# Four sets of expert-row buffers, a straight attention stage, and integer row numbers written by a reduction, in a graph-attention and mixture-of-experts kernel

## The reference

```python
def gnn(x, adj, W, a):                       # 4 heads of 32
    h = (x @ W).reshape(B, N, 4, 32).transpose(0, 2, 1, 3)
    s1, s2 = einsum('bhnd,hd->bhn', h, a1), einsum('bhmd,hd->bhm', h, a2)
    e = leaky_relu(s1[..., None] + s2[:, :, None, :], 0.2)
    e = where(adj[:, None] == 0, -inf, e)
    return softmax(e) @ h                    # back to 128 features

def ffn(x, Wg, bg, W1, b1, W2, b2):          # 8 experts, the best 2 of each token
    scores, idx = top_k(x @ Wg.T + bg, 2)
    p = softmax(scores)
    return sum over the 2 experts e of p_e * (relu(x @ W1[e].T + b1[e]) @ W2[e].T + b2[e])

x = x + gnn(layernorm(x), adj, W, a)
x = x + ffn(layernorm(x), Wg, bg, W1, b1, W2, b2)
```

## Time and profile before

| what | us |
|---|---|
| median of three runs | 736.47 (729.72 to 737.64) |
| the profiled execution | 735.45 |
| its span, first to last instruction | 733.6 |
| mean granted TensorE clock (share of full speed) | 0.852 |

### The profile page before, as it was taken

The page is one execution under the profiler, slowest core; times in us unless marked ns, Lnnn a source line. Parts: engine busy times, 40 slices in busy tenths (PEclk is TensorE's granted clock), DMA queues, the critical chain, the costliest instruction groups (busy, mean ns, idle before and its releaser), DMA issues.

```text
span 733.6 us, 23123 instructions
## 1 busy us (share of the span) xinstructions
PE 527.0 (72%) x7450; PEld 471.8 (64%) x7509; DVE 543.2 (74%) x1566; ACT 443.5 (60%) x908; POOL 430.7 (59%) x384
## 2 busy tenths in 40 slices
PE   1798878888887898886210888798888978888200
PEld 1598768887777888876210677687777867767100
DVE  4598999887999989988468566656746765666277
ACT  1788867756777786662132665566656656656064
POOL 2344487875888787786465166555655755564500
PEclk9999998968999888898655799999998999999755
DMA  8712122320333332000415222222222222221099
GB/s 308 270 60 60 60 84 78 88 84 23 86 86 86 83 79 83 25 28 31 143 40 106 60 68 70 74 67 63 79 64 65 75 68 61 69 71 49 7 356 331
DMA packets 60760, 67.64 MB, mean 92 GB/s; under 512 B 7266, under 2 KB 46317, under 8 KB 60416
## 3 DMA queue, kind: packets, MB, share of 16 engines
q1 hardware_dynamic: 41936, 44.31, 20.0%
q0 software_dynamic: 8816, 17.46, 7.3%
q10 hardware_dynamic: 9920, 4.73, 2.4%
HBM read 44.16 MB, written 23.22 MB: 92 GB/s over the span
## 4 chain that ended last, share of the span: by engine, by line
PE 47%; DVE 20%; issue 16%; DMA 6%; another core or an unknown queue 4%; ACT 4%; POOL 1%; DVEq 1%; ACTq 1%; SPq 0%; POOLq 0%
PE bank L1413 15%; PE bank L1401 13%; PE bank L1233 6%; PE bank L1224 3%; DVE bs L676 2%; PE bank L1389 2%; PE bank L1262 2%; DVE G L790 1%; DMA adji<-expert_out 1%; PE bank L1255 1%; DVE mv L679 1%; DVE T L799 1%; ACT G L549 1%; POOL expert_rows L467 1%
## 5 line engine op out<-in xcount | busy, mean ns | idle before, releaser
L517 POOL DMA_INDIRECT expert_out<-ysb,bidx x142 | 165.4, 1164 | 129.0 <-DVE ysb L1159 71.3
L467 POOL DMA_INDIRECT expert_rows<-rowt,idx x128 | 154.4, 1206 | 61.7 <-issue 34.5
L549 ACT ACTIVATE G<-bank,s2c 128x512 uint8<-128x512 f32 x256 | 154.3, 696 | 10.3 <-remote 9.8
L1233 PE MATMUL bank<-V,G 128*128 128x66 bf16 x3072 | 141.0, 202 | 14.5 <-issue 11.0
L1413 PE MATMUL bank<-W2h,G 128*128 x1704 | 122.6, 228 | 33.2 <-issue 29.9
L646 ACT ACTIVATE h<-bank,b1s,sc 128x256 f32<-128x256 f32 x284 | 138.0, 569 | 13.5 <-PE bank L1401 8.3
L1233 PEld LDWEIGHTS bank<-V,G 128*128 128x128 fp8e4 x3072 | 129.3, 103 | 18.5 <-issue 11.7
L1413 PEld LDWEIGHTS bank<-W2h,G 128*128 128x128 f16 x1704 | 107.2, 102 | 51.4 <-issue 50.2
L1401 PE MATMUL bank<-xt,W1h 128*128 128x256 f16 x852 | 113.5, 282 | 7.1 <-issue 6.7
L639 ACT ACTIVATE xt<-bank 128x512 f16<-128x512 f16 x71 | 43.0, 605 | 95.7 <-remote 79.3
L1142 DVE CAST G<-h 128x1024 f16<-128x1024 f32 x71 | 54.1, 762 | 58.9 <-ACT h L646 57.0
(11 more groups left out here) (159 smaller groups left out, 795.0 us busy)
## 6 DMA issues: line engine op xcount, KB each, us to landing
adji<-in_adj SPq DMA_DIRECT2D x16, 1024.0 KB
xb<-expert_rows SPq DMA_DIRECT2D x71, 130.0 KB
G<-in_L_ffn_W SPq DMA_DIRECT2D x2, 2048.0 KB, 9.3
adji<-expert_out SPq DMA_DIRECT2D x8, 512.0 KB, 5.6
G<-expert_out SPq DMA_DIRECT2D x8, 512.0 KB, 7.6
expert_out<-ysb,bidx POOLq DMA_INDIRECT x142
expert_rows<-rowt,idx POOLq DMA_INDIRECT x128
out<-adji ACTq DMA_DIRECT2D x8, 256.0 KB, 6.8
```

The source lines that it names most:

```text
L467: pool.indirect_dma_start(xs, bass.IndirectOffsetOnAxis(ap=idx[:, Z.p, k, j:j + 1], axis=0), rowt[:, Z.p, j, :], None).then_inc(scattered[ ...
L517: pool.indirect_dma_start(ybuf, bass.IndirectOffsetOnAxis(ap=bidx[:, B.o, t:t + 1], axis=0), ysb[:, B.q, t, :], None, bounds_check=2 * TOK ...
L549: act.activation(Gs[:, M.p, h // 2, mt, :, h % 2], zb[h][:, :], ACT.Sign, bias=s2c[:, M.p, mt, h:h + 1]).then_inc(S["z_used"], 1)
L1233: last = mm(o[:, h, :], G8[:, R.p, h // 2, mt, nt * P:(nt + 1) * P, h % 2], v[:, h, :], start=False, stop=(part == H and mt == NT - 1 and ...
```

## The change

What it does: `rowt` and `idx` get four sets instead of two, with four semaphores that count the scatters, and the waits for their reuse look four batches back. `slots` loses its loop; every slot of the attention stage is straight code on all four engines, so that every register expression in it becomes a constant. `slotf` and the step `indices` are gone: `places` reduces `prod` by a maximum straight into the int32 `idx`, after the wait for the scatters. The two copies into the row buffer become reductions by a maximum over a dimension of length one. `PLACE_STEPS` is 9, and two waits that count its steps follow. The expert stage and SP's own loop over the adjacency loads are as they were.

```diff
-LN_STEPS, ..., PLACE_STEPS = 8, 5, 2, 6, 2, 4, 13, 10
+LN_STEPS, ..., PLACE_STEPS = 8, 5, 2, 6, 2, 4, 13, 9
...
-        slotf = sb("slotf", [P, 2, NT])
-        idx = sb("idx", [P, 2, 2, NT], I32)
-        rowt = sb("rowt", [P, 2, NT, ROW])
+        idx = sb("idx", [P, 4, 2, NT], I32)
+        rowt = sb("rowt", [P, 4, NT, ROW])
...
-        scattered = [S["scattered0"], S["scattered1"]]
+        scattered = [S[f"scattered{k}"] for k in range(4)]
...
         def slots(eng, body, ahead, behind):
-            start = behind + 3
-            pairs = (NB - ahead - start) // 2
...
-            for s in range(-ahead, start):
-                body(fixed(s))
-            with eng.Fori(0, pairs) as i:
-                for u in range(2):
-                    body(looped(u, i))
-            for s in range(start + 2 * pairs, NB + behind):
-                body(fixed(s))
+            for s in range(-ahead, NB + behind):
+                at = lambda k, s=s: Batch(s + k) if 0 <= s + k < NB else None
+                at.s = s
+                body(at)
...
-            sp.wait_ge(scattered[0], 16 * 2 * NT * NB // 2)
-            sp.wait_ge(scattered[1], 16 * 2 * NT * NB // 2)
+            for k in range(4):
+                sp.wait_ge(scattered[k], 16 * 2 * NT * NB // 4)
...
             def weights(Z):
-                ge(act, S["place_steps"], Z.n * PLACE_STEPS - 4)
+                ge(act, S["place_steps"], Z.n * PLACE_STEPS - 3)
...
             def high_rows(Q):
-                ge(act, scattered[Q.p], Q.h * 16 * 2 * NT)
-                act.activation(rowt[:, Q.p, :, 0:D // 2].bitcast(FP16), xn2[:, :, :], ACT.Copy) \
+                ge(act, scattered[Q.q], Q.f * 16 * 2 * NT)
+                act.activation(rowt[:, Q.q, :, 0:D // 2].bitcast(FP16), xn2[:, :, :], ACT.Copy) \
...
             def places(Z):
-                pc.did(dve.tensor_reduce(slotf[:, :, :], prod[:, :, :, :], AX.X, ALU.add))
-                ge(dve, scattered[Z.p], Z.h * 16 * 2 * NT)
-                pc.did(dve.tensor_copy(rowt[:, Z.p, :, D + 1], v01[:, 0, :]))
-                pc.did(dve.tensor_copy(rowt[:, Z.p, :, D], C(C_TOK)[:, bass.ds(Z.n * NT, NT)]))
-
-            def indices(Z):
-                pc = Chain(dve, S["place_steps"], PLACE_STEPS, Z.n)
-                pc.k = 9
-                pc.after(7)
-                pc.did(dve.tensor_copy(idx[:, Z.p], slotf[:, :, :]))
+                ge(dve, scattered[Z.q], Z.f * 16 * 2 * NT)
+                pc.did(dve.tensor_reduce(idx[:, Z.q], prod[:, :, :, :], AX.X, ALU.max))
+                pc.did(dve.tensor_reduce(rowt[:, Z.q, :, D + 1], v01[:, 0, :].unsqueeze(2), AX.X, ALU.max))
+                pc.did(dve.tensor_reduce(rowt[:, Z.q, :, D], C(C_TOK)[:, bass.ds(Z.n * NT, NT)].unsqueeze(2),
+                                         AX.X, ALU.max))
...
                 if m1:
                     scaled_sums(m1, 0)
-                if m4:
-                    indices(m4)
```

More of the change, by code:

```diff
@@ L151 @@
 PIECES = 4
-LN_STEPS, S_STEPS, MX_STEPS, ARG_STEPS, X_STEPS, ATT_STEPS, ROUTE_STEPS, PLACE_STEPS = 8, 5, 2, 6, 2, 4, 13, 10
+LN_STEPS, S_STEPS, MX_STEPS, ARG_STEPS, X_STEPS, ATT_STEPS, ROUTE_STEPS, PLACE_STEPS = 8, 5, 2, 6, 2, 4, 13, 9
 def build(nc, x, adj, W, a, Wg, bg, W1, b1, W2, b2, const, out):
@@ L314, in build @@
             ln2 rstd2 nb2_ready xn2_ready x2T_ready xn2T_ready gate_ready route_steps dm_ready place_steps ed_ready rank_ready
-            hi_ready lo_ready scattered0 scattered1 tab_steps ends_ready tab_ready pads_ready
+            hi_ready lo_ready scattered0 scattered1 scattered2 scattered3 tab_steps ends_ready tab_ready pads_ready
             ld_rows0 ld_rows1 ld_rows2 ld_rows3 bt_ready xt_ready up_ready hid_ready split_steps down_ready y_ready
@@ L333, in slots @@
         def slots(eng, body, ahead, behind):
-            start = behind + 3
-            pairs = (NB - ahead - start) // 2
-            def fixed(s):
-                at = lambda k: Batch(s + k) if 0 <= s + k < NB else None
+            for s in range(-ahead, NB + behind):
+                at = lambda k, s=s: Batch(s + k) if 0 <= s + k < NB else None
                 at.s = s
[L339 to L344, removed]
-            for s in range(-ahead, start):
-                body(fixed(s))
-            with eng.Fori(0, pairs) as i:
-                for u in range(2):
-                    body(looped(u, i))
-            for s in range(start + 2 * pairs, NB + behind):
-                body(fixed(s))
+                body(at)
         def blocks(eng, body):
@@ L467, in scatter @@
                     pool.indirect_dma_start(
-                        xs, bass.IndirectOffsetOnAxis(ap=idx[:, Z.p, k, j:j + 1], axis=0),
-                        rowt[:, Z.p, j, :], None).then_inc(scattered[Z.p], 16)
+                        xs, bass.IndirectOffsetOnAxis(ap=idx[:, Z.q, k, j:j + 1], axis=0),
+                        rowt[:, Z.q, j, :], None).then_inc(scattered[Z.q], 16)
             def low_rows(Q):
                 hold(pool, S["hi_ready"], Q.n + 1, S["pool_turns"])
-                pool.tensor_tensor(rowt[:, Q.p, :, D // 2:D].bitcast(FP16), xn2[:, :, :],
-                                   rowt[:, Q.p, :, 0:D // 2].bitcast(FP16), ALU.subtract) \
+                pool.tensor_tensor(rowt[:, Q.q, :, D // 2:D].bitcast(FP16), xn2[:, :, :],
+                                   rowt[:, Q.q, :, 0:D // 2].bitcast(FP16), ALU.subtract) \
                     .then_inc(S["lo_ready"], 1)
@@ L828, in low_rows @@
                 dve.wait_ge(S["hi_ready"], Q.n + 1)
-                dve.tensor_tensor(rowt[:, Q.p, :, D // 2:D].bitcast(FP16), xn2[:, :, :],
-                                  rowt[:, Q.p, :, 0:D // 2].bitcast(FP16), ALU.subtract).then_inc(S["lo_ready"], 1)
+                dve.tensor_tensor(rowt[:, Q.q, :, D // 2:D].bitcast(FP16), xn2[:, :, :],
+                                  rowt[:, Q.q, :, 0:D // 2].bitcast(FP16), ALU.subtract).then_inc(S["lo_ready"], 1)
             def stats2(R, half):
```

## The result

Over 20 runs of each on one chip the changed kernel takes 725.87 us (median; 714.72 to 729.73), the kernel before 729.44 (724.42 to 737.64). The ratio is 0.9882, 95% interval 0.9853 to 0.9911: 8.6 us faster. The medians of all runs lie only 3.6 us apart. The forecast was 9 us. By the ratio the size came out; much of the way to it did not.

A forecast was written before the change was run, and what follows sets the result against it. No single engine led all twelve attention slots; DVE's copies waited for POOL. Slot gains, limited by POOL's and PE's own work, summed to 8.7 us, rounded 9: median 736.5 to 727.5 us, own range 721 to 733, 8 in 10 712 to 738.

The forecast's parts named there:

- reductions that do not wait: DVE's row edits: small reductions run undisturbed by GpSimd at 0.15 to 0.21 us each, argued from L983.
- rival D: DVE's new reductions wait as the copies did, so only the order changes: 736 us; chance 0.06.
- straight code at 0: Attention slots without the loop: register work saved is not visible, bounds -0.3 to +0.3 us for eight slots each.
- Rival C: Fetching straight code stalls PE, DVE or ACT from 150 to 318 us; 13 more pages cost 14 us: 742; chance 0.08.
- The walk of `edges` into `low_part`: DVE's L782 starts earlier and meets GpSimd's L457: up to some tenths of a microsecond per slot, not in the sum.
- the slots led by DVE: Attention slots where DVE was the chain: two like 215.87 give 1.4 us each, the one at 108.98 gives 1.9.
- the four PE-led ones: Four attention slots like the one at 276.50, bound by PE with its stalls: 0, at most 0.9 us each.
- The first slot: The attention slot at 89.09, where only the `idx` conversion stood: 19.89 to 18.4 us, a gain of 1.5.
- rival A: DVE and POOL led everywhere; PE's stalls and half clock come from late feeding; twelve slots give 28 us: 708; chance 0.22.
- the three waits of 7.4, 22.4 and 8.1 us: DVE's L985, L986 and L993 in the attention stage: 48 tiny instructions, 30.2 us of it standing still, 2.5 per slot.
- the four sets at 0: ACT's L598 waited 2.2 us in all for landed scatters; four sets give between 0 and 2.2 us, taken as 0.
- a sign against itself: A gain lying behind 340 us, after the attention stage, where the forecast gave nothing, would show it wrong.

The follow-up runs named there:

- The two halves: The kernel before with the int32 reduction alone, 1.0002, and the kernel before with the two row reductions alone, 0.9978; both on the second chip.
- the version at 0.972: The changed kernel with its two one-long reductions turned back into copies: 0.9722 to the kernel before on the third chip, 0.9813 on the fourth.

## Why the prediction was right, and where it was not

**Right.** The prices: reductions that do not wait, 0.21, 0.15 and 0.15 us; nothing more for an int32 result (rival D is out); GpSimd's wait for `idx` gone from the twelve slots; straight code at 0, shown alone at 0.997 where TensorE does not stall. DVE's busy time over twelve slots fell by 31.9 us, a little more than the 22 to 30 given. Rival C, code fetch, did not come: the instruction queue carries 66 packets in place of 52 (the forecast said some 13 more), and the one long "issue" wait, 5.6 us, stood in the kernel before as well. The walk of `edges` into `low_part`, no term of the sum, cost next to nothing on the two chips with stalls: L767 takes 1219 ns in the mean on the first, as before (1218), and 1318 on the second.

The proof that a reduction does not wait was weaker than it reads in the forecast. L983 starts 0.20 us after the scatter, and at 0.24 a copy doesn't wait either. The ten reductions named above, at 0.33 or 0.34 us, show it.

**Right in size, wrong in place: the sum slot by slot.** That 8.7 us of terms met a ratio worth 8.6 is luck in good part. The terms did not come where they stood, the medians of all runs differ by 3.6 us, and the forecast median of 727.5 lies near 725.87 in part because the kernel before came out at 729.44 over 20 runs, 7 us below the 736.47 that the sum started from.

The forecast took 1.4 to 1.9 us from the slots led by DVE and wrote "the four PE-led ones: 0, at most 0.9 each". The first slot stays at 20.0 us on both chips with stalls (19.89 in the earlier trace rows; 18.4 was forecast). On the second chip, against the version with the int32 reduction alone, the slots eight to eleven, led by PE in the kernel before, fall from 82.4 to 76.7 us, 1.4 each. On the first, against the kernel before, they fall by 2.0 in all. The step that failed is "That is why I let the PE-led slots stand": the edits do not touch the stalls, that held, but it does not follow that these slots stand. On the second chip the half clock behind the stalls is rarer, which is what rival A said, at part of its strength; that PE being fed earlier does it is argued here, not shown. In the profiled execution on the first chip the clock did not rise (0.84 after, 0.85 before), and what slots of 18.0 and 18.9 us gave, those of 24.5 with two stalls took back. Rival A's 708 did not come on either.

**Wrong: waits as terms to be added.** The forecast summed the three waits of 7.4, 22.4 and 8.1 us as if each were given back by its own edit. The single edits on the second chip say that they are nearly one: with the copies left, or with the conversion left, that one waits until `low_part` ends, and GpSimd's first scatter, which needs the row and the row number, waits for it. The two halves gave 0 and 0.2% alone. With all three gone, and four sets, it was 1.5%. That the wait moves is shown in the traces; that it is why the parts don't add up is the best reading, with numbers that clear the noise by little. Whether the three without the sets would give all of that where TensorE stalls was not tried.

**Wrong: the four sets at 0.** ACT's 2.2 us were read rightly in the trace of the chip with stalls, where the scatters have landed by the time they are asked for; but that reading does not carry to a faster chip. Without stalls two sets cost ACT 23.7 us of waiting. In time they seem to cost 1.2 to 1.3% (0.984 with two sets in three runs of two versions; 0.971 and 0.972 with four and one small part put back), but the version at 0.972 came out at 0.981 in its other run, and by that one it is 0.3%. Where TensorE stalls, the sets with the straight code gave 0.3%; the sets were not tried there without it.

**Open.** Of the 5.7 us between the two profiled executions 4.4 lie behind the attention stage, at 387 to 388 us, where the forecast gave 0 and named such a gain as a sign against itself. In the six profiles from chips with stalls the rest of the span takes 345.4, 346.2 and 346.7 us in the three kernels with a loop and 341.0, 342.3 and 342.6 in the three without; where there are no stalls it is 283.3 to 285.5 either way (one kernel with a loop, seven without). The difference lies between the first and the last scatter of the expert stage, whose code is the same: 274 to 276 us against 269 to 272. So the straight code may be worth up to 4 us behind its own stage on a stalling chip. Six profiles don't settle it. Nor was the changed kernel itself timed on a chip without stalls: that it would be near 0.97 there follows from its neighbours alone.

## What to carry to other kernels

When several small operations wait for the same long one on another engine, and that engine then waits for them, price them as one lock: removing all but one moves the wait to the last, and a test of a single edit can call each of them worthless. Ask what would stop a second engine at that place before adding up waits by line. And read a buffer's reuse wait together with what else slows the run: a wait of 0 in a trace says that something else is late, not that the buffers suffice.

## What the runs showed of the hardware

TensorE's stalls go with the chip. All six profiles from the first two chips have them, none of the eight from the other two, and the kernel before, the only one timed on both kinds, takes 729 to 736 us on the one and 662 on the other; no kernel was profiled on both. With the stalls the expert stage (142 scatters, the same code in all kernels) takes 269 to 276 us from its first to its last scatter; without them 213. PE's waits there, from 419 us on, in the kernel before on the first chip, and all that there are in the stage on the third chip (copies put back):

```profile
PE bank L1413 <- issue: 29.7, 56, 1.2
PE bank L1401 <- issue: 6.7, 13, 1.1
```

```profile
PE bank L1389 <- DVE ysb L1135: 1.4, 1, 1.4
```

That is 36.4 us of "issue" against none. PE is also granted 0.93 of its clock in that stage, and 0.99 without stalls, and is busy 225.4 us there against 203.6. The two make 58 of the 61 us by which the stage is longer, and the stage is most of the 74 us between the second chip and the third. What holds PE there no run showed; that indirect DMAs cause it was not tried.

The second surprise is that one small conversion (128x8 numbers), at the same place in DVE's queue, costs 0.41 us in a version on one chip and 1.50 in another version on another: what an operation that can wait for GpSimd costs is set by what GpSimd is doing when it comes.
